# Scores of a self attention: one float32 product, or three products of rounded high and low parts

## What is computed

```python
q = _apply_rotary(einsum(x, W_Q) + b_Q)          # 8 x 256 x 16 x 128
k = _apply_rotary(einsum(x, W_K) + b_K)
v = einsum(x, W_V) + b_V
scores = einsum(q, k) / sqrt(128)                # 256 x 256 per batch and head
scores = where(causal, scores, 0)
max_v = max(abs(scores), axis=-1)
attn_w = sign(scores) * exp(sign(scores) * scores - max_v)
attn = attn_w / (sum(abs(attn_w), axis=-1) + 1e-6)
out = einsum(einsum(v, attn), W_O) + b_O
```

## Time and profile before

| | us |
|---|---|
| median of 3 runs | 1519.03 (1518.56 to 1520.51) |
| the profiled execution, its own time | 1520.14 |
| its span, first to last instruction | 1517.1 |
| PE busy | 1397.2 (92%) |
| PEld busy | 1097.6 (72%) |
| DVE busy | 1219.8 (80%) |
| ACT busy | 802.9 (53%) |
| POOL busy | 668.4 (44%) |
| mean granted clock of TensorE | 0.973 |

### The profile page before, as it was taken

One profiled execution on the slowest core, in us unless ns is written; L12 is line 12 of the kernel. 1 busy time (PEld: TensorE's weight loads), 2 busy tenths in 40 slices (PEclk: granted clock), 3 DMA queues, 4 the chain that ended last, 5 costly groups with the idle time before them and its releaser, 6 DMA issues.

```text
span 1517.1 us, 25412 instructions
## 1 busy us (share of the span) xinstructions
PE 1397.2 (92%) x8594; PEld 1097.6 (72%) x8594; DVE 1219.8 (80%) x1990; ACT 802.9 (53%) x1798; POOL 668.4 (44%) x749
## 2 busy tenths in 40 slices
PE   5899999999999999999999999889999998359886
PEld 4788888888888888888888888776777776213332
DVE  6988888888888888888887888636788887669996
ACT  4444444445444443455465465445555555258884
POOL 4434335234334334443433432352345553448984
PEclk9999999999999999999999999989999999779998
DMA  5401101011010110021112010240000004014433
GB/s 209 157 11 42 46 25 42 28 43 42 28 43 23 38 52 15 15 70 57 36 42 91 28 63 29 70 126 15 15 15 15 14 0 172 3 30 92 91 85 93
DMA packets 73380, 79.93 MB, mean 53 GB/s; under 512 B 46006, under 2 KB 46518, under 8 KB 72892
## 3 DMA queue, kind: packets, MB, share of 16 engines
q1 hardware_dynamic: 73276, 78.73, 17.0%
HBM read 59.83 MB, written 8.40 MB: 45 GB/s over the span
## 4 chain that ended last, share of the span: by engine, by line
PE 50%; DVE 29%; issue 10%; POOL 7%; ACT 2%; DMA 1%; DVEq 1%; SPq 0%; POOLq 0%; ACTq 0%
PE psum L326 9%; PE psum L328 8%; PE psum L327 8%; DVE rope_b L513 6%; PE psum L939 4%; PE psum L940 3%; PE psum L941 3%; PE psum L367 3%; DVE p L522 3%; DVE total_e L526 3%; DVE acc L556 3%; DVE s L494 2%; PE psum L1007 2%; PE psum L388 2%; DVE rope_a L513 2%
## 5 line engine op out<-in xcount | busy, mean ns | idle before, releaser
L730 POOL TENSOR_TENSOR qk<-rope_a,rope_b 128x512 f32<-128x512 f32 x128 | 177.4, 1386 | 569.3 <-DVE rope_b L513 569.3
L326 PE MATMUL psum<-x_hi,w_hi 128*128 128x512 f32 x512 | 210.8, 412 | 11.4 <-POOL w_lo L724 11.4
L328 PE MATMUL psum<-x_hi,w_lo 128*128 128x512 f32 x512 | 201.7, 394 | 0.0
L327 PE MATMUL psum<-x_lo,w_hi 128*128 128x512 f32 x512 | 200.8, 392 | 0.0
L513 DVE SCALAR_TENSOR_TENSOR rope_b<-psum,qk_bias,sin 64x512 f32<-64x512 f32 x256 | 192.0, 750 | 3.7
L604 ACT ACTIVATE e<-s 128x384 f32<-128x384 f32 x128 | 66.4, 519 | 242.6 <-DVE s L494 242.6
L494 DVE SCALAR_TENSOR_TENSOR s<-psum,tri 128x384 f32<-128x384 f32 x128 | 70.8, 553 | 121.2 <-PE psum L367 121.2
L326 PE MATMUL psum<-w_hi,x_hi 128*128 128x256 f32 x512 | 147.4, 288 | 0.0
L327 PE MATMUL psum<-w_lo,x_hi 128*128 128x256 f32 x512 | 144.7, 283 | 0.0
L328 PE MATMUL psum<-w_hi,x_lo 128*128 128x256 f32 x512 | 144.6, 282 | 0.0
L618 ACT ACTIVATE e<-p 128x128 f32<-128x128 f32 x128 | 39.5, 309 | 184.2 <-DVE p L522 184.2
(11 more groups left out here) (183 smaller groups left out, 3796.3 us busy)
## 6 DMA issues: line engine op xcount, KB each, us to landing
stage<-w_self_dram SPq DMA_DIRECT2D x64, 256.0 KB, 2.9
w_raw<-w_ffn_dram SPq DMA_DIRECT2D x32, 512.0 KB, 3.6
acc<-xT_dram SPq DMA_DIRECT2D x4, 1024.0 KB, 7.6
acc<-x_dram SPq DMA_DIRECT2D x1, 4096.0 KB, 14.7
w_signs<-w_sign SPq DMA_DIRECT2D x16, 256.0 KB, 2.1
c_raw<-ctxT_dram SPq DMA_DIRECT2D x8, 512.0 KB, 3.6
xstage<-w_cross_dram SPq DMA_DIRECT2D x16, 256.0 KB, 3.0
w<-w_signs SPq DMA_DIRECT2D x2, 2048.0 KB, 12.1
```

The lines of the kernel that those rows point to most:

```text
L326: pe.matmul(ps, ah, bh, start=n == 0, stop=False)
L327: pe.matmul(ps, ah, bl, start=False, stop=False)
L328: last = pe.matmul(ps, al, bh, start=False, stop=n == len(pairs) - 1)
L730: nc.gpsimd.tensor_tensor(qk[:, k % 2, which, :], rope_a[:, which, :], rope_b[:, which, :], ALU.add).then_inc(qk_ready, 1)
```

## The change

q and k after the rotation are kept as a high and a low part, with one buffer each. POOL now adds rope_b into rope_a in place (`add_rope`), ACT rounds the sum to qk_hi (new `round_qk`), and POOL subtracts it from the sum to make qk_lo (new `split_qk`). Each batch's score, before two float32 products (128 and 256 columns), is now two times three products of float32r parts by the helper `three`. The lists of PE, DVE, ACT and POOL are changed as the diff shows.

```diff
--- before.py
+++ after.py
@@ -150,7 +150,8 @@
         v = sb("v", [P, 2, 4, 256])
         z_hi = sb("z_hi", [P, 2, 2, W], F32R)
         z_lo = sb("z_lo", [P, 2, 2, W], F32R)
-        qk = sb("qk", [P, 2, 2, W])
+        qk_hi = sb("qk_hi", [P, 2, W], F32R)
+        qk_lo = sb("qk_lo", [P, 2, W], F32R)
         rope_a = sb("rope_a", [P, 2, W])
         rope_b = sb("rope_b", [P, 2, W])
         cos = sb("cos", [P, S])
@@ -361,11 +364,11 @@
                 if b == 0:
                     pe.wait_ge(qk_ready, u * 2 + 2)
                 wait(pe, s_ready, (u - 1) * 2 + b + 1)
-                q, kk = qk[:, k % 2, 0, :], qk[:, k % 2, 1, :]
-                pe.matmul(psS[b][:, 0:P], q[:, b * S:b * S + P], kk[:, b * S:b * S + P],
-                          start=True, stop=True)
-                pe.matmul(psS[b][:, P:LW], q[:, b * S + P:(b + 1) * S], kk[:, b * S:(b + 1) * S],
-                          start=True, stop=True).then_inc(scores, 1)
+                near, far = slice(b * S, b * S + P), slice(b * S + P, (b + 1) * S)
+                three(psS[b][:, 0:P], [(qk_hi[:, 0, near], qk_lo[:, 0, near], qk_hi[:, 1, near], qk_lo[:, 1, near])])
+                both = slice(b * S, (b + 1) * S)
+                three(psS[b][:, P:LW], [(qk_hi[:, 0, far], qk_lo[:, 0, far], qk_hi[:, 1, both], qk_lo[:, 1, both])]
+                      ).then_inc(scores, 1)
 
             def turn(u, b):
                 if isinstance(u, int) and u == 0 and b == 0:
@@ -416,6 +419,8 @@
 
             def emit(t, k, i):
                 odd = k % 2 == 1
+                if live(t, 0):
+                    project(t, k, 0)
                 if live(t, 1):
                     score(t - 1, k - 1, 0)
                     score(t - 1, k - 1, 1)
@@ -423,21 +428,17 @@
                     pe.wait_ge(w_meaned, 1)
                 if live(t, 2):
                     turn(t - 2, 0)
-                if live(t, 0):
-                    project(t, k, 0)
-                if live(t, 2):
-                    turn(t - 2, 1)
                 if odd and o_live(t, k):
                     output(t, k, 0)
                 if live(t, 0):
                     project(t, k, 1)
-                if odd and o_live(t, k):
-                    output(t, k, 1)
+                if live(t, 2):
+                    turn(t - 2, 1)
+                if o_live(t, k):
+                    output(t, k, 1 if odd else 0)
                 if live(t, 2):
                     mix(t - 2, (k - 2) % 8, 0)
                     mix(t - 2, (k - 2) % 8, 1)
-                if not odd and o_live(t, k):
-                    output(t, k, 0)
                 if live(t, 0):
                     project_v(t, k)
                 if not odd and o_live(t, k):
@@ -559,15 +560,15 @@
                 odd = k % 2 == 1
                 if isinstance(t, int) and i == SCALED_IN and k == 0:
                     scale_weights()
-                if live(t, 1):
-                    mask_and_max(t - 1, 0)
-                    mask_and_max(t - 1, 1)
                 if live(t, 3):
                     z_low(t - 3, (k - 3) % 8)
                 if live(t, 1):
                     v_out(t - 1, (k - 1) % 8, v_bias[:, bass.ds(group(t, k, i, 1) * 256, 256)])
                 if odd and live(t, 5):
                     add_output(t - 1, (k - 1) % 8, 1)
+                if live(t, 1):
+                    mask_and_max(t - 1, 0)
+                    mask_and_max(t - 1, 1)
                 if live(t, 0):
                     rope(t, k, 0, bass.ds(group(t, k, i) * 2 + k % 2, 1))
                 if odd and o_live(t, k):
@@ -619,6 +620,11 @@
                 nc.scalar.activation(e[:, b, P:LW], p[:, b, P:LW], ACT.Abs, accum_out=total[:, b, 1:2]
                                      ).then_inc(total_ready, 1)
 
+            def round_qk(t, which):
+                act.wait_ge(qk_summed, t * 2 + which + 1)
+                wait(act, scores, (t - 1) * 2 + 2)
+                nc.scalar.copy(qk_hi[:, which, :], rope_a[:, which, :]).then_inc(qk_rounded, 1)
+
             def take_turned(u, b):
                 act.wait_ge(turned, u * 2 + b + 1)
                 wait(act, z_mm, u)
@@ -707,12 +713,16 @@
                     exps(t - 1, 1)
                 if live(t, 2):
                     take_turned(t - 2, 1)
+                if live(t, 0):
+                    round_qk(t, 0)
                 if live(t, 1):
                     totals(t - 1, 0)
                     totals(t - 1, 1)
                 if isinstance(t, int) and t + 2 < PAIRS:
                     round_x(t + 2)
                 ffn_pieces(t, k, i)
+                if live(t, 0):
+                    round_qk(t, 1)
 
             for t in range(UNITS + LAG):
                 emit(t, t % 8, (t - LAG) // 8 if LAG <= t < UNITS - 8 + LAG else None)
@@ -724,11 +734,15 @@
                 nc.gpsimd.tensor_tensor(w_lo[:, n, :], stage[:, n % STG, :], w_hi[:, n, :].bitcast(F32),
                                         ALU.subtract).then_inc(w_ready, 1)
 
-            def add_rope(t, k, which):
+            def add_rope(t, which):
                 pool.wait_ge(qk_turned, t * 2 + which + 1)
-                wait(pool, scores, (t - 2) * 2 + 2)
-                nc.gpsimd.tensor_tensor(qk[:, k % 2, which, :], rope_a[:, which, :], rope_b[:, which, :],
-                                        ALU.add).then_inc(qk_ready, 1)
+                nc.gpsimd.tensor_tensor(rope_a[:, which, :], rope_a[:, which, :], rope_b[:, which, :],
+                                        ALU.add).then_inc(qk_summed, 1)
+
+            def split_qk(t, which):
+                pool.wait_ge(qk_rounded, t * 2 + which + 1)
+                nc.gpsimd.tensor_tensor(qk_lo[:, which, :], rope_a[:, which, :], qk_hi[:, which, :].bitcast(F32),
+                                        ALU.subtract).then_inc(qk_ready, 1)
 
             def norm(u, b):
                 pool.wait_ge(inv_ready, u * 2 + b + 1)
@@ -755,14 +769,17 @@
                     next_pieces(t, k)
                 if isinstance(t, int) and t == 0:
                     split_low(Q1, 0)
-                    add_rope(t, k, 0)
+                if live(t, 0):
+                    add_rope(t, 0)
+                    split_qk(t, 0)
+                if isinstance(t, int) and t == 0:
                     split_low(K1, 0)
-                    add_rope(t, k, 1)
+                if live(t, 0):
+                    add_rope(t, 1)
+                    split_qk(t, 1)
+                if isinstance(t, int) and t == 0:
                     split_low(O0, 0)
                     split_low(O1, 0)
-                elif live(t, 0):
-                    add_rope(t, k, 0)
-                    add_rope(t, k, 1)
                 if live(t, 1):
                     norm(t - 1, 0)
                     norm(t - 1, 1)
```

More of the change, by code:

```diff
@@ L178, in self_attention @@
         qk_turned = sem("qk_turned")
+        qk_summed = sem("qk_summed")
+        qk_rounded = sem("qk_rounded")
         qk_ready = sem("qk_ready")
```

## The result

The changed kernel takes 1557.24 us (median of four runs, 1555.29 to 1559.98), the kernel before 1518.8 on the same chip: a ratio of 1.0253, 95% interval 1.0231 to 1.0275. The forecast was 1554, range 1540 to 1584. The profiled execution has a span of 1557.1 us (before 1517.1).

A forecast was written before the change was run, and what follows sets the result against it. PE leads, held up by DVE's late output addition in even slots. 32 us for 30 pairs plus 3 for group starts gave +35 on 1520.1, so 1555; the median being 1.1 lower, 1554, range 1540 to 1584.

The forecast's parts named there:

- The even slot: Self attention, DVE's path from project q to the addition, then output 1: 16.23 us against 14.97 before.
- The odd slot: Self attention, length set by PE's own work: 14.51 us in all.
- The loop: Self attention's 30 pairs of slots with outputs: 30.8 us a pair, 1.1 more, making 32 us.
- The group's start: Once a group, ACT rounds four weight pieces ahead of z_high, delaying DVE's mask 0.5 to 0.7 us; 3 us added.
- The scores' price: PE's twelve score products at 0.12 us each: 1.44 us a slot, 0.12 more; 1.20 at 0.08, 2.10 at 0.23.
- Rival 1: PE's scores: the short 128-column float32r product runs at float32's rate, 0.23 us, giving 1581; chance 0.20.
- The split at nothing: ACT's rounding and POOL's subtraction before the score cost nothing, project q covering them with 1.1 us left.
- Rival 3: Even slots: POOL's subtraction for q meets DVE's signs, lengthening one by about 1.1 us; 33 more, 1587; chance 0.05.
- Rival 2: DVE's even-slot path at least 1.7 us shorter, in time for the addition; 21 us less, 1498; chance 0.10.
- Rival 4, no change: Half the wait at output 1 is made up elsewhere and short products take 0.08: within 0.2%; chance 0.05.
- The wait's total: PE's waits for DVE's addition into acc: some 60 us in total instead of 29.

The follow-up runs named there:

- e1: Changed kernel with DVE's even-slot addition of output 0 moved from last step to right behind the two signs: 1503.76 us, 0.9888 of the kernel before.
- e2: Changed kernel with DVE's even-slot addition of output 0 moved between the rope of k and the two inversions: 1509.15 us, 0.9928 of the kernel before.
- e6: Changed kernel without the two additions of 1e-6 to the sums, the output addition still last in the even slot: 1508.08 us, 0.9936 of the kernel before.
- e3: Kernel before with only the changed lists of PE and DVE, q and k left float32, no split: 1548.74 us, 1.0183 of the kernel before.
- e4: Changed kernel with PE's and DVE's lists of the kernel before, so split and twelve products alone: 1549.88 us, 1.0195 of the kernel before.
- e5: Kernel before with the changed PE and DVE lists, float32 scores, and the even-slot output addition behind the signs: 1496.14 us, 0.9843 of the kernel before.
- e7: Kernel before with the even-slot addition of output 0 moved between the rope of k and the inversions: 1505.1 us, 0.9905 of the kernel before.

## Why the prediction was right

- *The even slot*: 16.23 by the sum, 16.18 measured. Its terms hold one by one: project q 2.72 (428.98 to 431.70 in the next slot), mask to addition 10.33 where the sum has 2.23 + 2.32 + 2.03 + 2.30 + 1.48 = 10.36, addition to output 0.75, output 1.49. That the path through DVE sets this slot is shown by e1, e2 and e6, which shorten it in three different ways.
- *The odd slot*: 14.51 + 0.1 by the sum, 14.61 measured. The scores in it are 0.06 too long, and hundredths in the other terms make it up; that the two agree to 0.01 is luck.
- *The loop*: +32, and 3 for the group's start, against 34.7 in the 60 slots. The pairs make 31 of it (30.77 less 29.74 for the usual ones, 30 times).
- *The group's start*: 7.7 us over the usual even slot in the changed kernel, for the seven groups together, against 0.9 in the kernel before. Its mechanism is as predicted, and the size near: in slot 24, whose first score starts at 382.71, four pieces on ACT stand before z_high, and DVE's mask starts 1.36 us behind that score instead of 0.89 (the two rows below). Such delays leave 2.9 of the 7.7. The other 4.8 are the three falls of the clock, which the sum didn't have. They are about made up by two things that it didn't have either: an odd slot of the kernel before (slot 53, 1.4 us over the usual) is a usual one now, and the last slot is 1.3 us shorter. So +35 is near the 34.7 in part by luck.

```profile
380.16 2.18 ACT L643 CAST w_hi<-stage 128x512 fp32r<-128x512 f32 x4 [0.21 <-PE psum L331]
```
```profile
384.07 0.55 DVE L495 SCALAR_TENSOR_TENSOR s<-psum,tri 128x384 f32<-128x384 f32 x1
```

- *The scores' price*: 0.12 was taken for the short product, between 0.08 and 0.23; three take 0.29, so 0.10 each. The slot's scores are 1.38 us, not 1.44. Rival 1 (1581) is out: this type isn't slowed to float32's rate at 128 columns. The Trainium skill, on the page TensorE: Matmul & The Clock Gate, section Back-to-back issue gap, gives 81 ns for 128 columns; the trace has 97.
- *The split at nothing*: right in the loop, where PE waits for qk_lo only at the start and the end. At the start it isn't nothing: the changed kernel's first score starts 4.5 us later than e3's (29.49 and 24.98), and its first addition 3.6. And e4 shows that it is free only because project q stands before the scores.
- *Rival 3, signs that stand behind the subtraction*: the changed kernel's signs take 968 ns in the mean, before 976. It doesn't happen.
- *Rival 2*: its condition, a path at least 1.7 us shorter, wasn't met. e6 takes one of its two stalls away, and with 1.34 us less in the path it is already faster than the kernel before.
- *Rival 4, no change*: out, as the interval starts at 1.0231.
- *What the sum didn't hold*: the rest of the program, which isn't changed, was 4.0 us longer in the profiled execution. With 34.1 in the loop (between additions) and 1.9 at the start it makes the span's 40.0. The forecast of 1554 is 3 us under the median of 1557 mainly because these weren't in it.
- *The wait's total* was put at some 60 us and is 54.1, since one such wait is 1.65 and not 1.7, and the other slots' waits have almost gone.

## What to carry to other kernels

When work is moved in lists written by hand, find the step whose result the bottleneck engine waits for, and count how late it comes from the start of the bottleneck's own slot; an order that hides one latency (here qk_lo) can expose another (here the output's addition). Compare slots of the usual length first, and then look at the unusual ones by themselves: here they held 5 us of another cause. A step that releases a shared bank belongs where its input is ready, not at the end of the list: two lines moved were worth 3.4% of the changed kernel's time here. And try a new order without the new arithmetic, since the good part of a combined change may be neither.

## What was not expected of the hardware

The unchanged feed forward ran at a lower granted clock in its first part. In the windows of 40 us that start 320 us after the last output addition (first the kernel before, then the changed one; the third number from the right is the clock):

```profile
1308.60:1348.60 40.00, 18.55 (x70) 9.28 (x70) 19.56 (x47) 9.75 (x16) 19.00 (x20) 0.66 0.07 13
```
```profile
1344.60:1384.60 40.00, 18.14 (x59) 8.96 (x59) 18.00 (x45) 7.40 (x14) 18.45 (x20) 0.59 0.05 10
```

PE is busy for less than half of these windows, and the mean of its two levels (1.2 and 2.4 GHz) is 0.66 and 0.59 of full speed; in the latter fewer products are done (59 against 70). e5 and e7 have 0.68 there, e4 0.66. The rest of the program varies by 5.6 us over the nine profiled executions (526.9 to 532.5). That a shift in time of the same work changes the clock it is granted fits this, but no run tests it, so it stays open. It is why differences of a few us here were read from the slots and not from the whole time.

The slots aren't free of the clock either, as the rows of slot 24 show. In the changed kernel PE waits about 1.9 us before output 1 in the first slot of most groups, and behind three of these waits the clock falls; behind waits of the same length in slots 8 and 16 it doesn't, and e5 has a wait of 2.56 us in slot 53 at a granted clock of 1.00. So a wait can cost more than its own length, but these runs don't tell when.

Another surprise: a reciprocal of 128x2 beside POOL's sum takes its normal time, while a TENSOR_SCALAR of the same size stands 0.9 us behind it (1.08 against 0.17). The kernel before already shows it. POOL's sum runs from 439.77 to 441.06, and the first reciprocal stands between the two total_e of the earlier trace rows:

```profile
439.93 0.17 DVE L530 RECIPROCAL inv<-total_e 128x2 f32<-128x2 f32 x1
```
```profile
L530 DVE RECIPROCAL inv<-total_e x128: 165/166/169, 38.2 to 973.8; 128x2 f32<-128x2 f32 x128
```

In the kernel before, 61 reciprocals start 0.15 to 0.16 us into such a sum, and none of all 128 takes over 0.169 us; 61 total_e start 0.23 to 0.25 us into one and take 1.05 to 1.09. The Trainium skill, on the page SBUF — State Buffer, section Who interferes with whom, names copy, cast and tensor_scalar as operations that can take the pair of ports shared with GpSimd, and doesn't name the reciprocal. The trace agrees for tensor_scalar.
